# First layer of a two-layer kernel: reciprocals of the softmax denominators on 128 partitions, and the LayerNorm mean taken out of the finishing chain

## The reference, cut to what matters

```
x_flat = x.reshape(B, C, H * W).transpose(0, 2, 1)
Q, K, V = split_heads(x_flat @ Wq + bq), split_heads(x_flat @ Wk + bk), split_heads(x_flat @ Wv + bv)   # 4 heads of 32
attn = softmax(einsum('bhnd,bhmd->bhnm', Q, K) * scale, axis=-1)
out = einsum('bhnm,bhmd->bhnd', attn, V)            # back to (B, 4096, 128)
y = out @ Wo + bo + x_flat
mu = mean(y, axis=-1); var = mean(square(y - mu), axis=-1)
y = (y - mu) / sqrt(var + 1e-5) * gamma + beta
```

## Time and profile before

| | value |
|---|---|
| time, median of 3 runs | 5652.98 us |
| the profiled execution's own time | 5656.6 us |
| span of its trace | 5654.8 us |
| PE, DVE, POOL, ACT busy in the span | 94%, 88%, 83%, 69% |
| granted TensorE clock, mean | 0.983 of full speed |
| maximum tiles reduced on DVE (L649) | 4096 x 682 ns |
| exponentials on ACT (L533) | 4096 x 600 ns |
| additions of pairs on POOL (L622, into `sums`) | 896 x 1282 ns |

### The profile page before, as it was taken

How to read it: one execution, slowest core, us unless ns; L and a number is a source line. 1 busy time by engine, 2 the same in 40 slices (tenths; PEclk the granted TensorE clock), 3 DMA queues, 4 the chain that set the end, 5 groups by cost and what they waited for, 6 DMA issues and landing times. The chain is left out here.

```text
span 5654.8 us, 81519 instructions
## 1 busy us (share of the span) xinstructions
PE 5338.5 (94%) x25264; PEld 2432.7 (43%) x25264; DVE 4949.7 (88%) x7220; ACT 3876.3 (69%) x7513; POOL 4692.7 (83%) x3661
## 2 busy tenths in 40 slices
PE   7999999999999999999999999968888888888888
PEld 3444444444444444444444444423333333333333
DVE  6888888888888888888888888829999999999998
ACT  3666666666666766666666666657777777777776
POOL 4888887888888788888788888747888888888887
PEclk8999999999999999999999999989999999999999
DMA  4111122211111211112211010225555555555555
GB/s 139 36 53 50 37 61 71 60 55 38 46 49 64 79 39 53 45 40 62 64 54 33 18 32 21 67 84 196 186 190 188 188 187 189 186 188 190 186 188 174
DMA packets 337475, 549.14 MB, mean 97 GB/s; under 512 B 76016, under 2 KB 99568, under 8 KB 335600
## 3 DMA queue, kind: packets, MB, share of 16 engines
q1 hardware_dynamic: 327536, 526.62, 28.8%
q10 hardware_dynamic: 9504, 17.31, 1.1%
HBM read 415.10 MB, written 109.84 MB: 93 GB/s over the span
## 5 line engine op out<-in xcount | busy, mean ns | idle before, releaser
L649 DVE TENSOR_REDUCE mpart<-ps 128x1 f32<-128x512 f32 x4096 | 2539.1, 682 | 536.4 <-PE ps L406 535.8
L533 ACT ACTIVATE exps<-ps 128x512 f32<-128x512 f32 x4096 | 2146.8, 600 | 1139.8 <-PE ps L413 1114.1
L406 PE MATMUL ps<-k_st,q_ring 96*128 96x512 f32 x4096 | 1778.2, 435 | 20.2 <-DMA k_st<-qk_split 15.6
L413 PE MATMUL ps<-q_ring,k_st 98*128 98x512 f32 x4096 | 1621.5, 397 | 3.8 <-ACT exps L533 3.4
L1300 POOL TENSOR_TENSOR hc<-hh,c_rep 128x512 f32<-128x512 f32 x1024 | 1295.8, 1278 | 310.8 <-DVE hh L1269 291.8
L1269 DVE TENSOR_TENSOR_SCAN hh<-d_a,carry,ps 128x512 f32<-128x512 f32 x1024 | 1311.9, 1284 | 0.0
L622 POOL TENSOR_TENSOR held<-exps 128x512 f32<-128x512 f32 x768 | 987.7, 1311 | 359.9 <-ACT exps L533 359.9
L406 PEld LDWEIGHTS ps<-k_st,q_ring 96*128 96x128 f32 x4096 | 774.7, 189 | 1136.5 <-DVE mpart L649 685.2
L622 POOL TENSOR_TENSOR sums<-exps 128x512 f32<-128x512 f32 x896 | 1134.5, 1282 | 72.0 <-ACT exps L533 70.0
L424 PE MATMUL ps<-exps,v_ring 128*32 128x512 f32 x8192 | 1092.4, 605 | 0.0
L413 PEld LDWEIGHTS ps<-q_ring,k_st 98*128 98x128 f32 x4096 | 778.3, 190 | 139.7 <-ACT exps L533 18.0
(11 more groups left out here) (113 smaller groups left out, 3881.3 us busy)
## 6 DMA issues: line engine op xcount, KB each, us to landing
d_a<-dt_dram SPq DMA_DIRECT2D x1040, 256.0 KB
qk_split<-hilo SPq DMA_DIRECT2D x128, 256.0 KB, 2.3
out_dram<-out_sb SPq DMA_DIRECT2D x128, 256.0 KB, 2.0
heads_in<-out_dram SPq DMA_DIRECT2D x32, 1024.0 KB, 5.2
q_ring<-qk_split SPq DMA_DIRECT2D x384, 64.0 KB, 2.0
k_st<-qk_split SPq DMA_DIRECT2D x45, 512.0 KB, 7.4
dt_dram<-dt SPq DMA_DIRECT2D x33, 512.0 KB, 5.5
s_u<-lo_u ACTq DMA_DIRECT2D x66, 256.0 KB, 5.9
```

The source lines that it names most:

```text
L406: nc.tensor.matmul(d_bank(("max", m, t)), q_ring[0:PARTS, m % 4, 128 * i:128 * i + 128], k_st[0:PARTS, g % 2, chunk(kc)], start=True, stop ...
L413: nc.tensor.matmul(a_bank(("exp", n, t)), k_st[0:SHIFT, n // NCH % 2, 128 * t:128 * t + 128], q_ring[0:SHIFT, n % 4, :], start=True, stop= ...
L533: nc.scalar.activation(exps[:, u % EXPS, CH * half:CH * half + CH], a_bank(("exp", n, t)), ACT.Exp, scale=SCALE).then_inc(a_done, 1)
L649: nc.vector.tensor_reduce(mpart[:, m % 2, t % 4, t // 4:t // 4 + 1], d_bank(("max", m, t)), AX.X, ALU.max).then_inc(d_done, 1)
```

## The change

1. **Denominators.** They are no longer stored into a tile and spread by a matmul. SP stores them in DRAM as 16-element pieces, loads them back so that 128 partitions hold 16 positions of one head each (with the four partial sums side by side), DVE adds the four and takes the reciprocal (128x16) in step 3, SP stores the result and loads it back spread over the partitions. Four more DMAs of a finishing slot take the place of a matmul and two activations.
2. **Mean.** `Wo` and `bo` are centred once (slot 6, step 2), so that out @ Wo + bo has mean 0 over channels. The mean of x comes as a 129th column beside `Wv`: the projection of V gives it, ACT copies it out of PSUM, SP stores it (512 elements of 4 bytes) and loads it spread over the partitions; POOL subtracts it from x (step 5). DVE adds that and the bias to the Wo product in one instruction; the matmul for the mean and one DVE instruction go. V takes two PSUM banks and two DVE instructions for it, since four times 129 columns don't fit one bank.
3. **Places.** Joining the heads and multiplying move from step 5 to 6, Wo from 6 to 7. ACT copies the denominators out after the first exponential of step 1, not after the fourth.

```diff
-                    add(d, ("value", p))
+                    add(d, ("value", p, 0))
+                    add(d, ("value", p, 1))
...
-                if v == 4:
-                    add(a, ("den", f))
+                if v == 7:
+                    add(d, ("wo", f))
                 if v == 6:
-                    add(d, ("wo", f))
-                if v == 7:
-                    add(d, ("mean", f))
-                if v == 5:
                     add(d, ("join", f))
...
-                    sp.wait_ge(d_done, d_at["value", p] + 1)
+                    sp.wait_ge(d_done, d_at["value", p, 1] + 1)
+                    sp.dma_start(mean_dram[p, :].rearrange("(j q o) -> q j o", j=4, o=1), mean_st[:, :].rearrange("q (j o) -> q j o", o=1), allow_slow_non_contiguous=True).then_inc(mean_stored, 16)
                     sp.dma_start(v_dram[b, :, :, 128 * c:128 * c + 128].rearrange("h p x -> p h x"),
                                  v_stage[:, :, :, :].rearrange("p h t d -> p h (t d)")).then_inc(v_stored, 16)
...
-                    sp.dma_start(denom[row:row + 4, half, :], den_parts[::D, n % 2, :]).then_inc(den_stored[n % 2], 16)
+                    if f >= 2 * NCH:
+                        sp.wait_ge(den_loaded, 16 * (f - 2 * NCH + 1))
+                    sp.dma_start(den_dram[batch_of(n) % 2, n % NCH, n // NCH % HEADS, :, :, :].rearrange("k q l -> q k l"),
+                                 den_parts[::D, n % 2, :].rearrange("q (k l) -> q k l", k=32)).then_inc(den_stored[n % 2], 16)
+                def load_den(f):
+                    sp.wait_ge(den_stored[f % 2], 16 * (last_slot(f) // 2 + 1))
+                    if f:
+                        sp.wait_ge(den_summed, f)
+                    sp.dma_start(den_in[:, :, :], den_dram[f // NCH % 2, f % NCH, :, :, :, :].rearrange("h k q l -> (h k) q l")
+                                 ).then_inc(den_loaded, 16)
+                def spread_rec(f):
+                    sp.wait_ge(rec_ready, f + 1)
+                    if f:
+                        sp.wait_ge(recip_ready, 16 * f)
+                        sp.wait_ge(d_done, d_at["join", f - 1] + 1)
+                    sp.dma_start(rec_dram.rearrange("h (k l) -> (h k) l", k=32), rec[:, :]).then_inc(rec_stored, 16)
+                    sp.wait_ge(rec_stored, 16 * f + 16)
+                    sp.dma_start(recip[:, :], rec_dram.rearrange("h (o l) -> h o l", o=1).to_broadcast([HEADS, D, CH])).then_inc(recip_ready, 16)
...
                     if f is not None:
                         if f:
-                            sp.wait_ge(d_done, d_at["wo", f - 1] + 1)
+                            sp.wait_ge(x_ready, f)
                         sp.dma_start(x_f[:, :], x[f // NCH, :, chunk(f % NCH)]).then_inc(f_in, 16)
+                        sp.wait_ge(mean_stored, 16 * f + 16)
+                        sp.dma_start(mean_x[:, :], mean_dram[f, :].rearrange("(o l) -> o l", o=1).to_broadcast([128, CH])).then_inc(f_in, 16)
...
+                    if f is not None:
+                        load_den(f)
                     if g is not None:
                         store_z(g)
+                    if f is not None:
+                        spread_rec(f)
...
-                def project_v(p):
-                    d_room(("value", p))
-                    for j in range(4):
-                        ins = nc.tensor.matmul(d_bank(("value", p))[:, 128 * j:128 * j + 128], xc[:, p % 2, 128 * j:128 * j + 128],
-                                               w_sb[:, 2, :], start=True, stop=True)
+                def project_v(p, part):
+                    key = "value", p, part
+                    d_room(key)
+                    for i, j in enumerate((range(3), (3,))[part]):
+                        ins = nc.tensor.matmul(d_bank(key)[:, (C + 1) * i:(C + 1) * i + C + 1], xc[:, p % 2, 128 * j:128 * j + 128],
+                                               wv[:, :], start=True, stop=True)
...
-                def spread_den(f):
-                    row, half = den_rows(f)
-                    pe.wait_ge(den_stored[f % 2], 16 * (last_slot(f) // 2 + 1))
-                    a_room(("den", f))
-                    nc.tensor.matmul(a_bank(("den", f)), sel_d[row:row + 16, :], denom[row:row + 16, half, :],
-                                     start=True, stop=True).then_inc(a_ready, 1)
...
-                def mean(f):
-                    pe.wait_ge(d_done, d_at["wo", f] + 1)
-                    d_room(("mean", f))
-                    nc.tensor.matmul(d_bank(("mean", f)), ones_c[:, :], y_sb[:, :], start=True, stop=True).then_inc(d_ready, 1)
...
+                def read_mean(p, part):
+                    n, j = ((3, 0), (1, 3))[part]
+                    key = "value", p, part
+                    act.wait_ge(d_ready, d_at[key] + 1)
+                    if p and part == 0:
+                        act.wait_ge(mean_stored, 16 * p)
+                    nc.scalar.copy(mean_st[:, j:j + n].rearrange("p (t o) -> p t o", o=1),
+                                   d_bank(key)[:, 0:n * (C + 1)].rearrange("p (t c) -> p t c", t=n)[:, :, C:C + 1]).then_inc(mean_read, 1)
...
-                def reciprocal(f):
-                    ready(("den", f))
-                    if f:
-                        act.wait_ge(d_done, d_at["join", f - 1] + 1)
-                    nc.scalar.activation(recip[:, :], a_bank(("den", f)), ACT.Ln).then_inc(a_done, 1)
-                    act.wait_ge(a_done, a_at["den", f] + 1)
-                    nc.scalar.activation(recip[:, :], recip[:, :], ACT.Exp, scale=-1.0).then_inc(recip_ready, 1)
...
+                            if v == 1 and t == 4 and n:
+                                read_den(n - 1)
...
+                def centre_x(f):
+                    pool.wait_ge(f_in, 32 * f + 32)
+                    if f:
+                        pool.wait_ge(d_done, d_at["wo", f - 1] + 1)
+                    pool.tensor_tensor(y_sb[:, :], x_f[:, :], mean_x[:, :], ALU.subtract).then_inc(x_ready, 1)
...
+                        if f is not None and v == 5:
+                            centre_x(f)
...
-                def values(p):
-                    ready(("value", p))
-                    if p:
+                def values(p, part):
+                    n, j = ((3, 0), (1, 3))[part]
+                    key = "value", p, part
+                    ready(key)
+                    dve.wait_ge(mean_read, 2 * p + part + 1)
...
+                def centre_weights():
+                    nc.vector.tensor_reduce(off[:, 0:1], w_sb[:, 3, :], AX.X, ALU.add).then_inc(off_ready, 1)
+                    nc.vector.tensor_reduce(off[:, 1:2], bo_sb[:, :], AX.X, ALU.add).then_inc(off_ready, 1)
+                    dve.wait_ge(off_ready, 2)
+                    nc.vector.tensor_scalar_mul(off[:, :], off[:, :], -1.0 / C).then_inc(off_ready, 1)
+                    dve.wait_ge(off_ready, 3)
+                    nc.vector.tensor_scalar(w_sb[:, 3, :], w_sb[:, 3, :], off[:, 0:1], None, ALU.add).then_inc(wo_ready, 1)
+                    nc.vector.tensor_tensor(bias[:, 2:3], bias[:, 2:3], off[:, 1:2], ALU.add).then_inc(wo_ready, 1)
+                def invert(f):
+                    dve.wait_ge(den_loaded, 16 * f + 16)
+                    if f:
+                        dve.wait_ge(rec_ready, f)
+                    nc.vector.tensor_reduce(den[:, :], den_in[:, :, :].rearrange("p q l -> p l q"), AX.X, ALU.add).then_inc(den_summed, 1)
+                    dve.wait_ge(den_summed, f + 1)
+                    if f:
+                        dve.wait_ge(rec_stored, 16 * f)
+                    nc.vector.reciprocal(rec[:, :], den[:, :]).then_inc(rec_ready, 1)
                 def normalise(f):
                     ready(("join", f))
-                    dve.wait_ge(recip_ready, f + 1)
+                    dve.wait_ge(recip_ready, 16 * f + 16)
                     nc.vector.tensor_tensor(normed[:, :], d_bank(("join", f)), recip[:, :], ALU.mult).then_inc(d_done, 1)
-                def add_x(f):
+                def centre(f):
                     ready(("wo", f))
-                    dve.wait_ge(f_in, 16 * f + 16)
-                    nc.vector.scalar_tensor_tensor(y_sb[:, :], d_bank(("wo", f)), bias[:, 2:3], x_f[:, :], ALU.add, ALU.add
-                                                   ).then_inc(d_done, 1)
-                def centre(f):
-                    ready(("mean", f))
+                    dve.wait_ge(x_ready, f + 1)
                     if f:
                         dve.wait_ge(squared, f)
-                    nc.vector.tensor_tensor(centred[:, :], y_sb[:, :], d_bank(("mean", f)), ALU.subtract).then_inc(d_done, 1)
+                        dve.wait_ge(scale_ready, f)
+                    nc.vector.scalar_tensor_tensor(centred[:, :], d_bank(("wo", f)), bias[:, 2:3], y_sb[:, :], ALU.add, ALU.add).then_inc(d_done, 1)
...
+                        if n == 6 and v == 2:
+                            centre_weights()
                         if g is not None and v == 2:
```

(42 more changed lines are left out.)

48 lines of the change are left out of this document (28 added, 20 removed).

## The result

The changed kernel takes 5722.47 us (median of 4 runs, 5715.31 to 5726.89), the kernel before 5653.82 (4 runs). The ratio is 1.0121, with a 95% interval of 1.0106 to 1.0136. The forecast was 5624, range 5602 to 5648: wrong in sign.

A forecast was written before the change was run, and what follows sets the result against it. DVE was taken to set the pace from step 3 on, PE following. -35.0 + 1 + 0.5 + 4 + 0.5 = -29 us gave 5627.6 for the profiled execution, 5624 as median; range 5602 to 5648.

The forecast's parts named there:

- Ahead of slot 0: Eight projections before slot 0, each with one more store on SP and waits for an ACT copy: +4 us, bounds 0 and 18.
- ACT loses two activations and isn't waited for.: Finishing slots: ACT has two activations fewer and no engine waits for it, so no cost was counted.
- 2.4 us to spare: Step 3 of finishing slots: denominators' load lands near 863.5, DVE wants it at 865.91, so no wait.
- rival 3: Finishing slots, step 3: denominators land late and DVE stands still; slower, 5674 us; chance 0.09.
- 1.60 - x ... 1.13 us a slot: Saving in each finishing slot beside exponentials, with DVE leading: 1.13 us, times 31 slots 35.0 us.
- x: DVE time of two added small instructions in step 3 of a finishing slot: 0.47 us, bounds 0.3 and 1.2.
- Rival 1: Finishing slots: PE is the bound and both removed matmuls are worth their length; 5595 us; chance 0.07.
- Rival 2: Finishing slots, step 3: the inversion is dear, at 1.2 us; 5647 us, no change that can be told; chance 0.15.
- The last chunk: The last finishing chunk, alone after the exponentials: later multiplication, no mean matmul; +0.5 us, bounds -3 and +4.
- Projecting slots: 24 slots with a projection, one more small DVE instruction each: 0.04 x 24 = +1 us, bounds 0 and 7.
- centring the weights: Five small DVE instructions, once: +0.5 us, bounds 0 and 1.5.

The follow-up runs named there:

- experiment 4: Changed kernel with the means turned by a PE transpose and stored as 4 pieces of 512 bytes: 5652.9 us, ratio 0.9999 to the kernel before.
- experiment 3: Kernel before plus an unread store per projection of 512 pieces, each in its own 64 bytes: 5655.8 us (4-byte pieces), 5655.5 us (64-byte pieces).
- experiments 5: Early copy of the denominators undone in the changed kernel: 5733.1 us; the same early copy added to the kernel before: 5674.4 us.
- experiment 6: Changed kernel with turned means and later denominators' copy: 5639.3 us; then also with the denominators' load ahead of the heads': 5624.2 us.
- experiment 7: Kernel with turned means, late copy and early denominators' load, DVE adding and inverting denominators only in the first finishing slot: 5612.6 us, ratio 0.9926.
- the final version: Changed kernel with turned means, later denominators' copy and the denominators' load ahead of the heads': 5624.2 us, ratio 0.9947 to the kernel before.

## Why the prediction was wrong

**The step that failed: "Ahead of slot 0 ... I take 8 x 0.5 = +4; bounds 0 and ... 18".** It measured +49.4 there, and another 16 us went in scattered slots. With the store mended and nothing else the kernel falls by 70 us, to the time of before [experiment 4]. The bound was built on a landing of 2.3 us for this store alone. The store took up to 11.8 (23.00 to 34.77), and the landing of all its neighbours in the rings grew with it. The rule of the Trainium skill for pieces under 512 bytes ("DMA: Bandwidth & Descriptors", "Specifications") that the prediction cites pointed the right way, and by it I named the upper bound as the one to take; even that was 18. A remedy by this rule works (experiment 4), but it asks for more than is needed here: 64-byte pieces, and even 4-byte pieces set apart, cost nothing that could be measured (experiment 3).

**"ACT loses two activations and isn't waited for."** Wrong. The copy moved ahead of three exponentials of step 1. I had looked at whose results they are, not at the ring of three banks: the extra matmul of step 1 is the fifth use there and needs the bank that the second exponential frees, which ACT now frees 0.47 us later (in the slot shown the copy stands at 922.33, the second exponential at 922.80). 0.39 us in each of 52 slots is 20 us. The step goes up and down with the edit both ways round (experiments 5 and 6); in the totals it was 20.2 us in the kernel before and 13.6 in the one with the turned means.

**"2.4 us to spare" for the denominators' load.** True in 28 of 31 slots, where DVE shows no wait for it in step 3. Wrong where a load of K opens the slot, in 32, 64 and 96. This is rival 3, with the mechanism named and the place missed: one slot stood for all 31, and it wasn't of the worst kind. What a late landing costs was mis-sized too: the prediction counts the standing, one for one, and leaves out the clock. DVE stood 2.33 us in slot 32, and the slot was 6.1 us longer than its neighbours at 30.60. The three slots lost 13.5 us against before; with the load moved up, they gain like the rest (experiment 6).

**"1.60 - x ... 1.13 us a slot".** Right, and so was the reason. x was 0.45 for 0.47, the slot without the other faults gains 31.42 - 30.20 = 1.22, and the inversion costs nearly its length: without it the slot gains 31.42 - 29.80 = 1.62, the forecast's 1.60 with x at nothing (experiment 7). Rival 1, both matmuls worth their length, falls: 2.06 was not to be had. Rival 2 falls as well: the reciprocal takes 0.25 us. Whether the iterative divide of which the Trainium skill speaks ("VectorE: DVE Perf Modes", "First, the fixed hardware budget") is part of that can't be told from this row: the reduction ahead of it takes as long, but reads four times as many elements.

**The last chunk, "+0.5 (bounds -3 and +4)".** The stretch from slot 127 on measured +5.0, of which `centred` came 3.9 later; the rest lies in the second layer, whose code is the same. The spread of the reciprocals landed after 5.1 us, for which the median of stores, 2.3, had stood. The counterpart of the earlier trace rows:

```profile
3826.53 0.69 DVE L739 TENSOR_TENSOR normed<-ps,recip 128x512 f32<-128x512 f32 x1 [6.55 <-DMA recip<-rec_dram]
3829.39 0.75 DVE L747 SCALAR_TENSOR_TENSOR centred<-ps,bias,y_sb 128x512 f32<-128x512 f32 x1 [2.17 <-PE ps L503]
```

From the multiplication to `centred` it is 2.86 us instead of 5.77, as the mean's matmul is gone; but the multiplication stands 45.4 us after the first exponential of slot 127 instead of 38.5, 6.8 more.

Projecting slots, apart from step 1, were as forecast, within 0.1 us; centring the weights cost 1.2 us for 0.5.

The terms nearly close. The profiled execution is 98 us over the forecast's 5627.6. Ahead of slot 0 that is 45 us over the +4 taken, 16 in scattered slots, 16 in the three slots (over their neighbours at 30.60), 20 in step 1 and 4.5 at the end: 102, less 3 that the finishing slots gained beyond the forecast and 2.6 of slot 126. That the final version lands on 5624, the forecast of the changed one, is chance in part: it has other edits, and its slots follow the same sum, but it lost nothing ahead of slot 0 for the +4 taken, and 3.7 at the end for the 0.5.

## What to carry to other kernels

Price an added DMA by what it does to the transfers around it, not only by a usual landing of its own, and look at where its pieces land: 2 KB in 4-byte pieces side by side cost 6 us a store where nothing covered them. When an instruction moves on an engine, follow the banks of its ring as well as its result. When one slot stands for many, take the one that opens with the largest transfers. A stall can cost more than its length, as the clock may fall behind it. And where the engine that leads is not the busiest, count the time on the one that leads.

## What the runs showed of the hardware

- 512 writes of 4 bytes to adjacent places in DRAM hold up what is in the rings with them: loads of 256 KB issued 1 us behind them landed after 11.4 us (3.7 before), and the writes themselves took up to 11.8 us to land. With 64 bytes between the starts of the pieces there was no measurable cost in 10 runs. As 128 pieces of 16 bytes the first exponential came 8.9 us late, against 49.4.
- A load whose outer dimension is 4 heads, spread over 128 partitions, took 5.1 us to be usable; four loads of 32 partitions took 3.6. While the one load moves (3722.1 to 3724.6 in the last kernel of experiment 6) the 16 DMA engines are busy for 24.6%, as 3.9 of them at work would be; with four loads (3722.9 to 3724.6) it is 47.4%. The Trainium skill, "DMA: Bandwidth & Descriptors", section "Why a DMA increments its semaphore by 16 and not by 1", says that the number of DMA engines follows from the slowest dimension of the pattern, at most 16; the 3.9 engines of the one load agree with this.
- A reciprocal of 128x16 on VectorE takes 0.25 us, as the reduction of 128x64 to 128x16 does.
- TensorE stood 2.69 us in slot 32, and its granted clock was 0.50 from 1087.8 to 1098.0, with matmuls of 0.63 us where they took 0.40; it then returned to 1.00. A step in that stretch took 5.57 us (1092.06 to 1097.63) instead of 3.25.
